# Splitting the row maxima after the transpose: the high part on ScalarE, the low part on VectorE out of PSUM, each stored by a DMA of its own

## The reference

```python
Q = (query @ Wq).reshape(b, q_len, G, Hpg, dh)
K = (key @ Wk).reshape(b, kv_len, G, dh)
V = (value @ Wv).reshape(b, kv_len, G, dh)
Q = Q / math.sqrt(dh)
scores = jnp.einsum('bqghd,bkgd->bghqk', Q, K)
scores = scores + m * rel[None, None, None]
scores = jnp.where(mask[:, None, None, None, :], scores, neg)
w = jax.nn.softmax(scores, axis=-1)
out = jnp.einsum('bghqk,bkgd->bqghd', w, V)
...
x = x + jnp.tanh(g_xattn[0]) * attention(layernorm(x), ctx)
x = x + jnp.tanh(g_ffn[0]) * quantised_ffn(layernorm(x))
```

## Time and profile before

| | |
|---|---|
| runs shown | 515.03, 527.6, 527.29 us; median 527.29 us |
| profiled execution | 515.34 us, its span 513.5 us |
| granted PE clock, mean over the span | 0.987 of full speed |
| busy: PE, DVE, ACT, POOL | 91%, 72%, 62%, 45% |
| attention steps 2 to 15 | from about 151.5 to 309 us |

### The profile page before, as it was taken

The page is one execution under the profiler, slowest core; times in us unless marked ns, Lnnn a source line. Parts: engine busy times, 40 slices in busy tenths (PEclk is TensorE's granted clock), DMA queues, the critical chain, the costliest instruction groups (busy, mean ns, idle before and its releaser), DMA issues.

```text
span 513.5 us, 8312 instructions
## 1 busy us (share of the span) xinstructions
PE 466.4 (91%) x2854; PEld 299.2 (58%) x2854; DVE 368.2 (72%) x674; ACT 320.5 (62%) x560; POOL 230.5 (45%) x250
## 2 busy tenths in 40 slices
PE   0699989999899999998899998988999999999966
PEld 0699989989875454554445554444444545555522
DVE  4778554448667887888978894377777778777762
ACT  0366626755656656666666666577777777777760
POOL 1100000000126787776362681057777777777630
PEclk9999998999999999999999999999999999999988
DMA  7879888899968889899676813014434333333323
GB/s 189 252 226 399 293 300 315 245 331 252 280 153 182 197 185 246 210 221 228 137 159 152 217 43 104 1 31 107 100 93 93 77 88 91 89 86 93 71 52 72
DMA packets 62834, 85.51 MB, mean 167 GB/s; under 512 B 37362, under 2 KB 48834, under 8 KB 61006
## 3 DMA queue, kind: packets, MB, share of 16 engines
q1 hardware_dynamic: 57614, 59.87, 47.3%
q0 software_dynamic: 3456, 12.58, 8.4%
q10 hardware_dynamic: 1728, 12.58, 7.0%
HBM read 57.94 MB, written 9.85 MB: 132 GB/s over the span
## 4 chain that ended last, share of the span: by engine, by line
PE 50%; DVE 15%; ACT 12%; DMA 12%; issue 6%; SPq 2%; ACTq 0%; POOL 0%; DVEq 0%; POOLq 0%
PE wide L1459 8%; DMA ct<-ctx_t 7%; PE bank L1288 6%; PE wide L1288 6%; PE bank L1381 5%; PE bank L1369 5%; PE bank L1329 5%; PE wide L1355 5%; PE bank L1469 5%; PE bank L1384 5%; DVE row_max L1021 3%; DMA qs<-nm_t 3%; ACT p_t L725 2%; DMA wq_f<-wq 2%; ACT act L837 2%
## 5 line engine op out<-in xcount | busy, mean ns | idle before, releaser
L1021 DVE TENSOR_REDUCE row_max<-wide 100x2 f32<-100x722 f32 x128 | 109.9, 903 | 21.0 <-PE wide L1355 20.0
L725 ACT ACTIVATE p_t<-bank 121x400 f32<-121x400 f32 x192 | 91.5, 506 | 52.5 <-PE bank L1369 49.3
L1459 PE MATMUL wide<-w_q,xq 128*128 128x512 bf16 x384 | 86.9, 380 | 2.7 <-DVE h L1139 2.4
L576 POOL TENSOR_TENSOR z<-h,lnw 128x512 f32<-128x512 f32 x48 | 61.1, 1275 | 15.2 <-DVE h L1139 14.6
L1459 PEld LDWEIGHTS wide<-w_q,xq 128*128 128x128 bf16 x384 | 35.5, 98 | 51.6 <-DVE h L1139 8.0
L1369 PE MATMUL bank<-qs,ks 103*121 103x400 f32 x144 | 52.0, 390 | 8.1 <-ACT p_t L725 5.5
L530 POOL DMA_DIRECT2D quant_in<-w_ffn x24 | 14.3, 597 | 98.0 <-PE bank L1329 91.5
L1329 PE MATMUL bank<-wv_f,ct 128*121 128x128 f32 x384 | 46.3, 278 | 4.0 <-DMA ct<-ctx_t 4.0
L968 DVE TENSOR_TENSOR ctl<-ct,cth 128x1445 fp32r<-128x1445 f32 x16 | 26.6, 1664 | 31.3 <-ACT cth L635 31.3
L1469 PE MATMUL bank<-w_q,yq 128*128 128x512 bf16 x192 | 46.5, 396 | 1.8 <-DMA yq<-y_int 1.7
L1329 PEld LDWEIGHTS bank<-wv_f,ct 128*121 128x121 f32 x384 | 45.4, 189 | 4.6 <-DMA ct<-ctx_t 4.6
(11 more groups left out here) (160 smaller groups left out, 920.5 us busy)
## 6 DMA issues: line engine op xcount, KB each, us to landing
quant_in<-w_ffn POOLq DMA_DIRECT2D x24, 512.0 KB, 6.4
ct<-ctx_t SPq DMA_DIRECT2D x16, 722.0 KB, 10.6
abs_b<-w_ffn ACTq DMA_DIRECT2D x7, 1024.0 KB, 10.1
ks<-k_all SPq DMA_DIRECT2D x36, 181.0 KB
q_scratch<-qhl SPq DMA_DIRECT2D x16, 400.0 KB, 5.9
abs_a<-w_ffn ACTq DMA_DIRECT2D x5, 1024.0 KB, 6.6
qs<-q_scratch SPq DMA_DIRECT2D x12, 400.0 KB
xb<-x SPq DMA_DIRECT2D x12, 256.0 KB, 2.9
```

Source lines behind the costliest of these rows:

```text
L576: nc.gpsimd.tensor_tensor(z[par][0:rows, c], h[0:rows, c], lnw[0:rows, c], ALU.mult).then_inc(z_done, 1)
L725: nc.scalar.activation(p_t[:, j, :], bank[j % 2][0:KT, 0:HQ], ACT.Exp).then_inc(exp_done, 1)
L1021: nc.vector.tensor_reduce(row_max[b % 2][:, 2 * u:2 * u + 2], wide[u % 2][0:SQ, :, 0:SK], AX_X, ALU.max).then_inc(s_maxed, 1)
L1459: mm = nc.tensor.matmul(wide[j % 2][0:rows, m, :], xq[par][:, c, 0:rows], w_q[:, m * C + c, 512 * j:512 * j + 512], start=(c == 0), stop=( ...
```

## The change

PE transposes the unsplit maxima, 16 rows of 100 in place of 32. ACT copies them from PSUM with a factor -1 to `nm_h`, rounding to the high part, and signals `nm_high`. DVE takes the negated maxima from the same place in PSUM, subtracts `nm_h`, writes `nm_l` and signals `nm_low`. SP stores the high row when `nm_high` comes and the low row when `nm_low` comes. `split_max` and its 32 instructions are gone. `low_max(b-1)` stands behind the third row maximum (u = 2) of step b; `low_max(0)` stands in context step 12, `low_max(15)` behind the attention steps. What waited for `nm_ready` waits for `nm_low`; POOL's `late_rows` no longer waits for the split of batch 1.

```diff
--- before.py
+++ after.py
@@ -162,8 +162,8 @@
     assert r_x <= end_a
     xh, xl = [xh0, xh1], [xl0, xl1]
     xt = [xt0, xt1]
-    nm_q = new("nm_q", [SQ, 2 * H], F32R)
-    nm_t = new("nm_t", [2 * H, SQ], F32R)
+    nm_h = new("nm_h", [H, SQ], F32R)
+    nm_l = new("nm_l", [H, SQ], F32R)
     row_max = [new(f"row_max{i}", [SQ, H], F32) for i in range(2)]
     inv_sum = new("inv_sum", [P, HQ], F32)
     sum_kept = new("sum_kept", [P, HQ], F32)
@@ -280,7 +280,7 @@
 
         qk_in = [sem(f"qk_in{i}") for i in range(SLOTS)]
         s_done, s_maxed = sem("s_done"), sem("s_maxed")
-        nm_split, nm_turned, nm_ready, nm_in = sem("nm_split"), sem("nm_turned"), sem("nm_ready"), sem("nm_in")
+        nm_turned, nm_high, nm_low, nm_in = sem("nm_turned"), sem("nm_high"), sem("nm_low"), sem("nm_in")
         st_done, exp_done = sem("st_done"), sem("exp_done")
         pv_done, o_ready = sem("pv_done"), sem("o_ready")
         log_ready, inv_ready, newton_step = sem("log_ready"), sem("inv_ready"), sem("newton_step")
@@ -326,7 +326,7 @@
 
         def turned_at(b):
 
-            return wide[1][0:2 * H, 0, 400:400 + SQ] if b == 0 else bank[2][0:2 * H, 400:400 + SQ]
+            return wide[1][0:H, 0, 400:400 + SQ] if b == 0 else bank[2][0:H, 400:400 + SQ]
 
         def qk_count(b):
 
@@ -389,10 +389,10 @@
 
             def store_max(b):
 
-                sp.wait_ge(nm_ready, b + 1)
-                for part in range(2):
+                for part, (split, nm) in enumerate(((nm_high, nm_h), (nm_low, nm_l))):
+                    sp.wait_ge(split, b + 1)
                     sp.dma_start(qs[b % SLOTS][ROWS_S + part:ROWS_S + part + 1, :, :].bitcast(F32).rearrange("p g (h q) -> p (g h) q", h=HPG),
-                                 nm_t[H * part:H * part + H, :].bitcast(F32)).then_inc(nm_in, 16)
+                                 nm[:, :].bitcast(F32)).then_inc(nm_in, 16)
 
             def load_qk(b):
 
@@ -518,7 +518,6 @@
             def late_rows():
 
                 pool.wait_ge(kl_ready, B)
-                pool.wait_ge(nm_split, 4)
                 nc.gpsimd.tensor_copy(qs_late[96:101, :, :], qs[0][96:101, :, :]).then_inc(late_set, 1)
                 nc.gpsimd.tensor_copy(ks_late[96:103, :, :], ks[0][96:103, :, :]).then_inc(late_set, 1)
                 pool.wait_ge(late_set, 2)
@@ -728,7 +727,7 @@
                 act.wait_ge(nm_turned, b + 1)
                 if b > 0:
                     act.wait_ge(nm_in, b * 32)
-                copy_high(nm_t[:, :], turned_at(b)).then_inc(nm_ready, 1)
+                copy_high(nm_h[:, :], turned_at(b), scale=-1.0).then_inc(nm_high, 1)
 
             def keep_pv(b):
 
@@ -1018,17 +1017,17 @@
 
             def largest_scores(b, u):
                 dve.wait_ge(s_done, b * PAIRS + (u + 1))
+                if b >= 2 and u == 0:
+                    dve.wait_ge(nm_turned, b - 1)
                 nc.vector.tensor_reduce(row_max[b % 2][:, 2 * u:2 * u + 2], wide[u % 2][0:SQ, :, 0:SK], AX_X, ALU.max).then_inc(s_maxed, 1)
 
-            def split_max(b):
-
-                dve.wait_ge(s_maxed, b * PAIRS + PAIRS)
+            def low_max(b):
+
+                dve.wait_ge(nm_high, b + 1)
                 if b > 0:
-                    dve.wait_ge(nm_turned, b)
-                nc.vector.tensor_scalar(nm_q[:, 0:H], row_max[b % 2][:, :], -1.0, None, ALU.mult).then_inc(nm_split, 1)
-                dve.wait_ge(nm_split, b * 2 + 1)
-                nc.vector.scalar_tensor_tensor(out=nm_q[:, H:2 * H], in0=row_max[b % 2][:, :], scalar=-1.0,
-                                               in1=nm_q[:, 0:H].bitcast(F32), op0=ALU.mult, op1=ALU.subtract).then_inc(nm_split, 1)
+                    dve.wait_ge(nm_in, b * 32)
+                nc.vector.scalar_tensor_tensor(out=nm_l[:, :], in0=turned_at(b), scalar=-1.0, in1=nm_h[:, :].bitcast(F32),
+                                               op0=ALU.mult, op1=ALU.subtract).then_inc(nm_low, 1)
 
             def normalise(b, step):
 
@@ -1051,12 +1050,12 @@
                 ctx_step(b)
                 if b == 1:
                     constant_rows(2)
+                if b == 12:
+                    low_max(0)
                 if b in SCORES_AT:
                     old, first = SCORES_AT[b]
                     for u in range(first, first + 2):
                         largest_scores(old, u)
-                if b == 11:
-                    split_max(0)
             def normalise_last():
 
                 dve.wait_ge(o_copied, B * 2)
@@ -1065,15 +1064,15 @@
                 o = o_t[:, :, (B - 1) * SQ:B * SQ]
                 nc.vector.tensor_tensor(o, o, inv_sum[:, :].rearrange("p (h q) -> p h q", h=HPG), ALU.mult).then_inc(o_ready, 1)
 
-            split_max(1)
             weight_scales()
             for b in range(2, B):
                 for u in range(PAIRS):
                     largest_scores(b, u)
+                    if u == 2:
+                        low_max(b - 1)
                     if b >= 3:
                         for step in NORMALISE_BEHIND.get(u, ()):
                             normalise(b - 3, step)
-                split_max(b)
                 if b == 10:
                     dve.wait_ge(wo_high, 1)
                     nc.vector.tensor_tensor(wo_l[:, :, :], wo_f[:, :, :], wo_h[:, :, :].bitcast(F32), ALU.subtract).then_inc(wo_low, 1)
@@ -1214,6 +1213,7 @@
                     second_sublayer(t - 1, 1 - par)
 
 
+            low_max(B - 1)
             residual(0, 0, 0)
             x1_stats(0, 0)
             nc.vector.tensor_copy(ident_b[:, :], ident[:, :]).then_inc(ident_set, 1)
@@ -1349,7 +1349,7 @@
                 if b > 0 or u > 1:
                     pe.wait_ge(s_maxed, b * PAIRS + (u - 1))
                 if b == 1 and u == 1:
-                    pe.wait_ge(nm_ready, 1)
+                    pe.wait_ge(nm_low, 1)
                 for k in range(2):
                     g, h = divmod(2 * u + k, HPG)
                     mm = nc.tensor.matmul(wide[u % 2][0:SQ, k, 0:SKP], qs[b % SLOTS][0:ROWS_S, g, h * SQ:(h + 1) * SQ],
@@ -1374,7 +1374,7 @@
                 n = KT_USED[kt]
                 pe.wait_ge(exp_done, b * UNITS + G * (kt + 1))
                 if kt == 0:
-                    pe.wait_ge(nm_ready, min(b + 2, B))
+                    pe.wait_ge(nm_low, min(b + 2, B))
                     if b > 0:
                         pe.wait_ge(o_copied, b * 2)
                 for g in range(G):
@@ -1386,10 +1386,12 @@
                 mm.then_inc(pv_done, 1)
 
             def turn_maxima(b):
-                pe.wait_ge(nm_split, b * 2 + 2)
+                pe.wait_ge(s_maxed, b * PAIRS + PAIRS)
+                if b >= 1:
+                    pe.wait_ge(nm_low, b)
                 if b >= 2:
                     pe.wait_ge(o_copied, (b - 2) * 2 + 1)
-                nc.tensor.transpose(turned_at(b), nm_q[:, :].bitcast(F32), ident[0:SQ, 0:SQ]).then_inc(nm_turned, 1)
+                nc.tensor.transpose(turned_at(b), row_max[b % 2][:, :], ident[0:SQ, 0:SQ]).then_inc(nm_turned, 1)
 
             def behind(b, u):
 
@@ -1438,7 +1440,7 @@
 
             def first_turn_xq():
                 pe.wait_ge(xq_rounded, 1)
-                pe.wait_ge(nm_ready, B)
+                pe.wait_ge(nm_low, B)
                 pe.wait_ge(ident_set, 1)
                 dst = wide[1][:, 0, :].bitcast(BF16)
                 low = xq_f[:, :].bitcast(BF16)
```

## The result

The changed kernel takes 528.07 us (median of 20 runs, 521.41 to 537.77), the kernel before 522.42 in 20 runs beside it (515.03 to 530.97). The ratio is 1.0122, with a 95% interval of 1.0091 to 1.0153: slower by 1.2%, and within 2%. A second set of 12 runs gave 1.0083 [1.0040, 1.0125].

A forecast was written before the change was run, and what follows sets the result against it. PE, busy 91% of the span, was taken to bound the kernel. -2.7 + 6.8 + 1.4 + 0 = +5.5 us took the profiled 515.34 to 520.8 and the median 527.29 to 532.8 us (+1.0%), range 515 to 536.

The forecast's parts named there:

- The level: Whole kernel: median of before, 527.29 us, taken as the upper of two levels 12 us apart, giving 532.8 us.
- Removed, -2.7: DVE's split of the maxima, two instructions per batch: its long cases on the chain go, saving 2.7 us.
- The low part, 0.26: New DVE instruction, 16 partitions x 100 columns, one input in PSUM: 0.26 us each, bounds 0.17 and 1.03.
- rival (c): On DVE, the hold-up moves from the split to the low part, 1.03 us each: 543.6 us; chance 0.02.
- The wait in each step, +6.8: Attention steps: PE waits for the low part before the values matmuls, 0.53 us in 12 steps, 6.8 in all.
- rival (a): Attention steps: new waits don't show, low part in time or PE makes delay good; 524.6 to 526 us; chance 0.15.
- Context step 12, +1.4: scores(1, 1): low_max(0) stands behind the keys' low part on DVE, so PE waits 1.4 us more.
- The second store, 0 with +0.9 and -1.4: Low row's store is issued later in attention steps: no net cost, bounds +0.9 and -1.4 us.
- Rival (b): At scores_t(b-1, 0), each step waits for the low row's landing: slower by over 2%, 551.7 us; chance 0.07.
- Rival (d): Attention steps: all the split's DVE time, 11.5 us, comes off the path: faster by over 2%, 515.8 us; chance 0.03.

The follow-up runs named there:

- the pair with and without it: Changed kernel with both moves and POOL's late copies held back, with the old split's two DVE instructions put back unread (1.0057) and without them (1.0023).
- the other pair: Changed kernel with the old split's two DVE instructions put back unread, 1.0220 of the kernel before, beside the changed kernel of the same set, 1.0083.
- both moves: Changed kernel with the low part behind u = 1 and batch 0's low part ahead of context step 12's DVE work: 0.9988 of the kernel before, 520.06 us.

## Why the prediction was right

The forecast was +5.5 us; the medians differ by 5.65, and the ratio makes 6.4 of 522.42; at equal clock the second set has 4.9. In the traces the steps are 7.2 and 6.6 us longer (two profiles) and the context part 4.0 and 4.2, 11 in all; that is against a profile of before with little in it that went wrong, and I use the traces for the terms, the ratios for the whole. The mechanism was right; that the total came out within 1 us is partly luck: half clock, which the sum does not have, and delay that is made good again, which it puts at nothing, work against each other. The range of 515 to 536 was so wide that no change at all would have been inside too. By its own steps:

**The level.** This was wrong. "The upper of two levels 12 us apart" was read into three runs. From the median of before that 20 runs give, the same sum leads to 527.9, where 528.07 was measured; the forecast of 532.8 was 4.7 too high for no reason of the change.

**Removed, -2.7.** Right in sign, as far as the runs can tell. The hold-up of the split by POOL is shown. Its price by the pair with and without it is 1.8 us by the ratios, with intervals that overlap, and 2.9 at equal clock, give or take 1.9; by the other pair it is 7.2 by the ratios, in a kernel whose late copies collide with it too.

**The low part, 0.26.** Measured 0.240, and never over 0.251 in any run, so rival (c) is out. The estimate of 0.23 worked out from the Trainium skill's "VectorE: DVE Perf Modes", section on the TRN2 errata, was the closer one, 0.01 from the measured value.

**The wait in each step, +6.8.** Right in mechanism, place and size: PE idles 6.7 us ahead of L1381, 12 times 0.50 plus 0.4 and 0.3. The step grew by 0.58, not 0.53. Undoing it takes the steps back to 10.56, and the wait alone makes them 11.14. In whole times the two experiments give 3.5 us (one undone) and 3.8 us (one alone, with an interval from 1.0 to 6.5). At equal clock they are 4.5 and 3.8. The traces suggest where a part of the rest is: PE waited 3.9, 6.0, 3.8 and 2.1 us for stores of maxima in the four kernels whose low part comes in time, and 0.5 to 4.0 in the six whose values matmuls wait; the two traces without half clock in the steps are 4.0 us apart, with 2.7 more of such waits in the shorter one. So rival (a) may have a grain of truth, some of the delay is made good behind it, but that is argued from single traces with overlapping ranges, and its mechanism, that the waits don't show, is not it. Half clock blurs the rest: the traces of the kernels with one and both moves have 13.7 and 13.5 us of it in the 13 steps. No term of the prediction was for the clock.

**Context step 12, +1.4.** Right: PE starts 1.59 behind ACT's copy in place of 0.14, 1.45 more, in both profiles and in three of other kernels that have the low part there. That the whole wait grew by only 0.97 and 1.25 is the copy's doing, which came a little sooner behind the transpose. What was missing is that both profiles then have PE at half clock for most of 7 us, some 3.0 us more. Whether that counts in the medians is not settled: the wait alone costs 0.9%, but 0.6 us at equal clock, and moving batch 0's low part ahead gave no gain that shows (1.0117 where the changed kernel has 1.0083, and 0.9988 where the kernel without that move has 1.0017; all the intervals overlap). In the second pair's profile the wait was still 2.6, through ACT's copy.

**The second store, 0 with +0.9 and -1.4.** The waits for landings went from 2.2 us to 3.0 and 4.0 in the two profiles: +0.8 and +1.8, near and beyond the upper bound. Four stood in the chain of the first profile. Rival (b) did not come: its mark was a mean of 4.75, and the low row's landings have a mean of 4.0 and 4.3 in the two profiles. The kernel with both moves and the late copies held had a mean of 4.8 and paid for it in seven small waits, 3.8 us, not in every step.

**Rival (d).** The row of the maxima shows what became of DVE's 11.3 us: its idle time ahead of the maxima went from 21.0 to 40.5 us. Where the waits are undone the floor of a step is 10.56 as before, not less.

## What to carry to other kernels

When a small result moves from one engine to another, look first at what stands ahead of it in the new engine's list and who waits behind it: here 0.24 us of work, one maximum too late in the list, cost PE 0.5 us in each step, and moving one line gave it back. When a buffer is shared by columns, every reader added becomes a wait for the writer of the other columns. When such a wait is to be measured, take the time from the end of what was waited for before to the start, not the length of the idle time, which also has in it how late everything else was. And take a kernel's spread from more than three runs before reading levels into it, with the granted clock of each run beside its time; one profile can show a gain of 4.7 us that the runs don't.

## What the hardware showed that I had not expected

**The clock behind a wait of PE.** The same pair of matmuls in context step 12 came behind waits of different length. Behind 0.4, 0.6, 0.7, 1.5 and 2.1 us the granted clock was 1.00 over the next 7 us. Behind 2.4, 2.6 and 2.9 us (three kernels) it was 0.76 over 7 us, behind 2.5, 2.8 and 3.3 us (the changed kernel twice, and the one with both stores late) 0.55, 0.56 and 0.59; in these three it fell before the wait was over. In one kernel, the one with the low part one pair earlier, it was 1.00 behind 2.9, so the length of the wait is not the whole rule. In the attention steps of these traces it also fell 0.3 to 1.7 us behind waits of 1.0 to 1.1 (in five of them). These are twelve executions of eleven kernels; no experiment varied the wait alone in steps.

**The landing of a small store** (of the low row; of both rows in kernels with one copy of both) moved with the kernel around it: a median of 3.5 to 4.0 us in the six profiles whose values matmuls wait, and 4.0, 4.4, 4.8 and 4.4 in the four that have the change without that wait (3.6 and 4.0 in the two of the kernel before and its copy with one wait). Whether the load of the DMA engines or the moment of the issue sets it was not measured by itself.

**The end of a reduction.** PE goes on 0.26 us behind the recorded end of a maximum out of PSUM where it waits for it (the kernel before with the wait alone), and 0.10 behind that of the low part (the changed kernel). An allowance of 0.05 for the semaphore, as in the prediction, was too small for both.
